# State-space input stage: softplus as one activation from PSUM, du per chunk, constants first, loops written out

## The reference

```
# state-space block (m0 and m1), 256 inner channels, 16 states
u, z    = split(x @ W_in)
u       = silu(causal_conv4(u))
dt,B,C  = split(u @ W_x)                     # 8, 16, 16 columns
delta   = softplus(dt @ W_dt + b_dt)
A       = -exp(A_log)
h[t]    = exp(delta[t]*A) * h[t-1] + delta[t]*u[t]*B[t]
y[t]    = sum over states of h[t]*C[t]  + u[t]*D
out     = (y * silu(z)) @ W_out

# mixture of experts (e0 and e1), 8 experts, the best 2 of each token
topv, topi = top_k(x @ Wg.T, 2);  w = softmax(topv)
comb       = one_hot(topi) weighted with w   # [tokens, 8]
```

## Time and profile before

| | us |
|---|---|
| median of three executions | 2250.76 |
| the profiled execution's own time | 2255.21 |
| its span, first to last instruction | 2253.4 |
| TensorE busy | 1847.1 (82%) |
| VectorE busy | 1723.9 (77%) |
| ScalarE busy | 1102.9 (49%) |
| GpSimd busy | 463.3 (21%) |
| granted TensorE clock, mean | 0.926 |

### The profile page before, as it was taken

The page is one execution under the profiler, slowest core; times in us unless marked ns, Lnnn a source line. Parts: engine busy times, 40 slices in busy tenths (PEclk is TensorE's granted clock), DMA queues, the critical chain, the costliest instruction groups (busy, mean ns, idle before and its releaser), DMA issues. The chain is left out here.

```text
span 2253.4 us, 48041 instructions
## 1 busy us (share of the span) xinstructions
PE 1847.1 (82%) x18116; PEld 897.4 (40%) x18116; DVE 1723.9 (77%) x3657; ACT 1102.9 (49%) x2023; POOL 463.3 (21%) x342
## 2 busy tenths in 40 slices
PE   6377777999479999998699964777685999999957
PEld 2122235344235555554434321222342555555524
DVE  5999975555679999993655469999766899999745
ACT  5433322322328778787222263333152777887825
POOL 2566641000200000000100025766431000000012
PEclk9699998999769999999799987999886999999978
DMA  3121201000111222212100001212003132222110
GB/s 104 42 82 67 82 30 57 1 0 0 56 47 41 51 52 52 46 36 34 58 0 0 0 8 49 84 65 78 25 1 106 26 55 60 52 50 50 30 16 19
DMA packets 43053, 96.50 MB, mean 43 GB/s; under 512 B 14153, under 2 KB 18189, under 8 KB 41438
## 3 DMA queue, kind: packets, MB, share of 16 engines
q1 hardware_dynamic: 41694, 91.04, 15.7%
q10 hardware_dynamic: 1152, 2.64, 0.3%
HBM read 75.42 MB, written 17.04 MB: 41 GB/s over the span
## 5 line engine op out<-in xcount | busy, mean ns | idle before, releaser
L1805 ACT ACTIVATE a1hd_probs<-a1hd_ps_k 128x512 f32<-128x512 f32 (+3 forms) x640 | 302.2, 543 | 118.2 <-PE a1hd_ps_k L1703 79.1
L1805 ACT ACTIVATE a0hd_probs<-a0hd_ps_k 128x512 f32<-128x512 f32 (+3 forms) x640 | 302.3, 543 | 117.0 <-PE a0hd_ps_k L1703 79.8
L1685 PE MATMUL a0hd_ps_q<-a0hd_k_op,a0hd_q_op 72*32 72x512 bf16 (+3 forms) x2560 | 270.5, 368 | 27.9 <-DMA a0hd_k_op<-a_k_parts 18.1
L1685 PE MATMUL a1hd_ps_q<-a1hd_k_op,a1hd_q_op 84*32 84x512 bf16 (+3 forms) x2560 | 270.3, 368 | 27.8 <-DMA a1hd_k_op<-in_alibi_k 18.1
L1763 DVE TENSOR_REDUCE a0hd_maxes<-a0hd_ps_q 128x1 f32<-128x512 f32 x384 | 252.1, 685 | 24.8 <-PE a0hd_ps_q L1685 21.7
L1763 DVE TENSOR_REDUCE a1hd_maxes<-a1hd_ps_q 128x1 f32<-128x512 f32 x384 | 252.2, 685 | 24.6 <-PE a1hd_ps_q L1685 21.2
L1699 PE MATMUL a1hd_ps_k<-a1hd_q_op,a1hd_k_op 87*32 87x512 bf16 (+3 forms) x2560 | 262.5, 352 | 7.4 <-ACT a1hd_probs L1805 4.9
L1699 PE MATMUL a0hd_ps_k<-a0hd_q_op,a0hd_k_op 75*32 75x512 bf16 (+3 forms) x2560 | 262.2, 352 | 6.5 <-ACT a0hd_probs L1805 4.9
L1033 ACT ACTIVATE e_silu<-e_psg,e_me_b 128x512 f32<-128x512 f32 x128 | 87.9, 687 | 256.7 <-PE e_psg L947 256.7
L1146 DVE SCALAR_TENSOR_TENSOR e_mid<-e_psv,e_me_b,e_silu 128x512 f32<-128x512 f32 x128 | 95.8, 750 | 108.6 <-PE e_psv L949 104.8
L608 POOL TENSOR_TENSOR m1sc_read<-m1sc_state,m1sc_c_rows 128x1024 f32<-128x1024 f32 x64 | 150.1, 2356 | 76.8 <-DVE m1sc_state L580 51.5
(11 more groups left out here) (349 smaller groups left out, 3322.7 us busy)
## 6 DMA issues: line engine op xcount, KB each, us to landing
m0sc_c_rows<-m_c_rows SPq DMA_DIRECT2D x32, 512.0 KB, 3.5
m1sc_c_rows<-m_c_rows SPq DMA_DIRECT2D x32, 512.0 KB, 3.6
a_oT<-a_outputs SPq DMA_DIRECT2D x32, 256.0 KB
a0hd_q_op<-a_q_parts SPq DMA_DIRECT2D x16, 288.0 KB
a0hd_k_op<-a_k_parts SPq DMA_DIRECT2D x16, 288.0 KB
a_outputs<-a0hd_o_sb SPq DMA_DIRECT2D x256, 18.0 KB
a1hd_q_op<-a_q_parts SPq DMA_DIRECT2D x16, 288.0 KB
a1hd_k_op<-a_k_parts SPq DMA_DIRECT2D x16, 288.0 KB
```

Of the source, the lines that this page charges most:

```text
L1685: last = pe.matmul(ps_q[32 * r:32 * r + 32, bank, 0:width], q_op[k % SLOT][0:NR, part(t, r)], k_op[k % SLOT][0:NR, kc * CH:kc * CH + width ...
L1805: act.activation(probs[:, n % PSLOT, 0:width], ps_k[:, n % KB, 0:width], ACT.Exp).then_inc(exp_done, 1)
```

## The change

In `mamba_inputs`:

- delta is one ScalarE activation, Softplus with the bias, straight from the dt bank, per chunk and channel half. `e`, the absolute value, max(dt,0), exp, ln, the rounding remainder and all additions to delta are gone, on all three engines.
- The dt products stand at the end of `items`: both halves of chunks 0 and 1, the xd product of chunk 3, then chunks 2 and 3. ScalarE does softplus of chunk 0 in step 5 ahead of the xd copy of chunk 3, and those of chunks 1, 2 and 3 after the steps, with the second bf16 part of chunk 3 between 1 and 2.
- du is made by VectorE alone, one product per chunk (1024 elements per partition).
- exp(A_log) is ScalarE's first instruction; its negation and the two instructions for diag_d stand in VectorE's step 0, behind the first normalisation.
- The DRAM rows hold B and C (32 rows a chunk, not 16); the scan reads the C rows from row 16 on.

In `mamba_scan` the loops are written out: the same steps in the same order on each engine, with constant targets and slices. In `moe` the loop over chunks is written out too, and the choice of experts is made by comparisons over all 2048 tokens at once: equal to the best value, times a row 8..1, maximum over the experts, equal to that row; the second with one more comparison that takes the first out. The row `iota` holds 8..1 in place of 0..7.

```diff
 def mamba_inputs(...)
-        for s in range(STEPS):
+        for s in range(NC + 1):
             items += [("u", s, h) for h in range(NH2) if s < NC]
-            items += [("dt", s - 3, h) for h in range(NH2) if s >= 3]
-            items += [("xd", s - 2, 0)] if 2 <= s < NC + 2 else []
-            items += [("gate", s - 1, h) for h in range(NH2) if 1 <= s <= NC]
-        late = {"u": 0, "gate": 1, "xd": 2, "dt": 3}
-        reader = {"u": raw_copied, "xd": xd_ready, "dt": relu_done, "gate": gate_ready}
+            items += [("xd", s - 2, 0)] if s >= 2 else []
+            items += [("gate", s - 1, h) for h in range(NH2) if s >= 1]
+        items += [("dt", c, h) for c in range(2) for h in range(NH2)]
+        items += [("xd", NC - 1, 0)]
+        items += [("dt", c, h) for c in range(2, NC) for h in range(NH2)]
+        reader = {"u": raw_copied, "xd": xd_ready, "dt": delta_ready, "gate": gate_ready}
...
 scalar
+            def second(c):
+                act.wait_ge(rest_ready, c + 1)
+                act.activation(parts[:, 1, chunk(c)], rest[:, c % 2, :], ACT.Copy).then_inc(split_1, 1)
+            def softplus(c):
+                for h in range(NH2):
+                    act.wait_ge(made, product_made("dt", c, h))
+                    act.activation(delta[:, h, chunk(c)], bank("dt", c, h), ACT.Softplus,
+                                   bias=w["dt_b"][:, h:h + 1]).then_inc(delta_ready, 1)
             act.wait_ge(w.loaded, w.full)
-            for s in range(STEPS):
+            act.activation(neg_a[:, :, :], w["a_log"][:, :, :], ACT.Exp).then_inc(a_exp, 1)
+            for s in range(NC + 2):
...
-                if s >= 3:
-                    ... Abs of dt (2 halves), second part of chunk s-3
+                if s >= 3 and s < NC + 2:
+                    second(s - 3)
+                if s == NC + 1:
+                    softplus(0)
...
-            ... exp of both halves, ln of both halves
+            softplus(1)
+            second(NC - 1)
+            softplus(2)
+            softplus(3)
 vector
                 if s == 0:
                     dve.wait_ge(padded, 1)
                     dve.wait_ge(w.loaded, w.full)
+                    dve.wait_ge(a_exp, 1)
+                    link(dve.tensor_scalar(neg_a[:, :, :], neg_a[:, :, :], -1.0, None, ALU.mult))
+                    for h in range(NH2):
+                        link(dve.tensor_scalar(diag_d[:, h, :], g["ident"][:, :], w["d"][:, h:h + 1], None, ALU.mult))
...
-            ... relu of dt, neg_a, diag_d, round_sum, lost_in_rounding, delta + ln, times_u(1)
+            for c in range(NC):
+                dve.wait_ge(delta_ready, NH2 * (c + 1))
+                dve.tensor_tensor(du[:, :, chunk(c)], delta[:, :, chunk(c)], u[:, :, chunk(c)], ALU.mult).then_inc(du_ready, 1)
 gpsimd
-                if s == NC + 1:
-                    lost_in_rounding(pool, 0)
-            times_u(pool, 0)
 sync
-                sp.dma_start(c_dram[:, chunk(c)], xd[RANK + NS:XDBL, chunk(c)]).then_inc(c_stored, 16)
+                sp.dma_start(bc_dram[:, chunk(c)], xd[RANK:XDBL, chunk(c)]).then_inc(c_stored, 16)

 def mamba_scan(...)
-            with eng.Fori(1, NS // 2) as i:
-                for s in range(2):
-                    step(k, i + k * (NS // 2), s)
+            for q in range(STEPS):          # on every engine, constant waits and slices
...
 def moe(...)
-                for i in range(NT):
-                    dve.wait_ge(maxed, i + 1)
-                    dve.max_index(index[:, i, :], best[:, i, :], logits[:, i, :]).then_inc(indexed, 1)
+            def find_index(k, marks):
+                last_first = g["iota"][:, :].unsqueeze(1).broadcast_to([P, NT, NE])
+                link(dve.tensor_tensor(marks[:, :, :], logits[:, :, :], spread(best[:, :, k:k + 1], NE), ALU.is_equal))
+                if k:
+                    link(dve.tensor_tensor(marks[:, :, :], marks[:, :, :], is0[:, :, :], ALU.is_gt))
+                link(dve.tensor_tensor(marks[:, :, :], marks[:, :, :], last_first, ALU.mult))
+                link(dve.tensor_reduce(rank[:, :, k:k + 1], marks[:, :, :], AX.X, ALU.max))
+                link(dve.tensor_tensor(marks[:, :, :], last_first, spread(rank[:, :, k:k + 1], NE), ALU.is_equal))
...
-            find_index()
+            find_index(0, is0)
             make_mid(0, 4, 4)
             make_mid(0, 5, 5)
-            mark()
+            find_index(1, is1)
...
-            with pe.Fori(1, NC - 1) as c:   # the same on scalar and vector
-                body(c, True)
-            body(NC - 1, False)
+            for c in range(1, NC):
+                body(c, c + 1 < NC)
```

More of the change, by code:

```diff
@@ L283, in _ @@
             pe.wait_ge(w.loaded, w.full)
-            for s in range(STEPS):
-                if s < NC:
-                    norm.turn(pe, s)
-                for k, (what, c, h) in enumerate(items):
-                    if c + late[what] != s:
-                        continue
+            for k, (what, c, h) in enumerate(items):
+                    if what == "u" and h == 0:
+                        norm.turn(pe, c)
                     if k >= RING:
@@ L325, in _ @@
                                        ACT.Copy).then_inc(raw_copied, 1)
-                if s >= 3:
-                    c = s - 3
-                    for h in range(NH2):
-                        act.wait_ge(made, product_made("dt", c, h))
-                        act.activation(e[:, h, chunk(c)], bank("dt", c, h), ACT.Abs,
-                                       bias=w["dt_b"][:, h:h + 1]).then_inc(abs_done, 1)
-                    act.wait_ge(rest_ready, c + 1)
-                    act.activation(parts[:, 1, chunk(c)], rest[:, c % 2, :], ACT.Copy).then_inc(split_1, 1)
+                if s >= 3 and s < NC + 2:
+                    second(s - 3)
+                if s == NC + 1:
+                    softplus(0)
                 if 2 <= s < NC + 2:
@@ L460, in _, with mamba_scan @@
             sp.wait_ge(g.late.loaded, g.late.full)
-def mamba_scan(nc, g, tag, u, delta, du, bc3, c_dram, neg_a, diag_d, gate):
+def mamba_scan(nc, g, tag, u, delta, du, bc3, bc_dram, neg_a, diag_d, gate):
     with ExitStack() as ctx:
@@ L485, in mamba_scan, with time, rows @@
         NB = SCT // CH
+        STEPS = NSC * NS
         block = ctx.enter_context(nc.Block())
[L488 to L506 removed]
+        def time(q, first=0, last=SCT):
+            return slice(q // NS * SCT + first, q // NS * SCT + last)
         @block.tensor
         def _(pe):
[L510 to L511 removed]
+            def rows(q):
                 for h in range(NH2):
[L513 removed]
+                    if q:
+                        pe.wait_ge(scanned, NH2 * (q - 1) + h + 1)
                     for b in range(NB):
[L515 to L517 removed]
+                        last = pe.matmul(drive[:, h, chunk(b)], g["sel"][:, q % NS, :], bc3[:, time(q, b * CH, (b + 1) * CH)],
+                                         start=True, stop=True)
+                    last.then_inc(rows_spread, 1)
             def skip(k):
@@ L529, in sum_states @@
                     for b in range(NB):
-                        last = pe.matmul(psy[:, h, chunk(b)], g["ident"][:, :], read[s][:, h, chunk(b)],
-                                         start=False, stop=ends, skip_group_check=True)
+                        last = pe.matmul(psy[:, h, chunk(b)], g["ident"][:, :], read[q % 2][:, h, chunk(b)],
+                                         start=False, stop=q % NS == NS - 1, skip_group_check=True)
                     last.then_inc(summed, 1)
-            def middle(k, r, s):
-                rows(k, r, s)
-                sum_states(r * 2 + (s - 1), 1 - s, False)
@@ L586, in times_gate @@
                     dve.wait_ge(summed, NS * NH2 * (k + 1) - (NH2 - 1 - h))
-                    dve.tensor_tensor(gate[:, h, tokens], psy[:, h, :], gate[:, h, tokens], ALU.mult).then_inc(gated, 1)
-            step(0, 0, 0)
-            for k in range(NSC):
-                step(k, k * (NS // 2), 1)
-                other_pairs(dve, k, step)
-                if k + 1 < NSC:
-                    step(k + 1, (k + 1) * (NS // 2), 0)
-                times_gate(k)
+                    dve.tensor_tensor(gate[:, h, time(NS * k)], psy[:, h, :], gate[:, h, time(NS * k)], ALU.mult).then_inc(gated, 1)
@@ L612, in _ @@
         @block.sync
         def _(sp):
[L614 to L619 removed]
+            for q in range(STEPS):
+                if q >= 2:
+                    sp.wait_ge(read_ready, NH2 * (q - 1))
+                sp.dma_start(c_rows[q % 2][:, :], bc_dram[NS + q % NS:NS + q % NS + 1, time(q)].broadcast_to([P, SCT])).then_inc(c_loaded[q % 2], 16)
@@ L926, in tokens @@
             def tokens(c):
-                return chunk(c) if isinstance(c, int) else ds(c * CH, CH)
+                return chunk(c)
             def product(c, e):
@@ L1059, in _ @@
             tail(0, True)
-            with act.Fori(1, NC - 1) as c:
-                body(c, True)
-            body(NC - 1, False)
```

(7 more changed lines are left out.)

185 lines of the change are left out of this document (47 added, 138 removed).

## The result

The changed kernel takes 2200.59 us, median of four executions (2200.30 to 2204.75), against 2250.14 for four of the kernel before on the same chip. The ratio is 0.978, with a 95% interval of 0.977 to 0.980. The forecast was 2197.7 in a range of 2191 to 2209; its sum had said 53.1 us, and the gain is 49.5 by the medians, 50.5 by the two profiled executions (own time 2204.75, span 2202.9). The mechanism and the place were right; one term, the block of m1, was 4 us too large.

A forecast was written before the change was run, and what follows sets the result against it. VectorE was taken to bound the input block's end. Savings of 25.5 + 25.5 + 1.0 - 0.45 + 1.6 = 53.1 us, against the median 2250.8, gave 2197.7; the 8-in-10 range was 2191 to 2209.

The forecast's parts named there:

- The place: End of the input block: VectorE, running without a gap from 62.04 to 87.98, was said to hold up the scan.
- The end of the block, m0: Input block of m0: to end at 62.4 instead of 87.98, 25.5 us less.
- the working: Part-by-part costing of the input block's new end; SiLU of chunk 3 to start of scan came to 12.8 us.
- The end of the block, m1: Input block of m1: the same 25.5 us less, as it repeats m0 row by row.
- dt 0, dt 1, xd 3 at 1.95 each: TensorE near the block's end: three products in turn from 49.4, 1.95 us each, done at 55.2.
- the stacking DMA: End of the input block: stacking of B and C lands last, at 62.4, 0.6 us behind du.
- Softplus, 1.28 a pair: ScalarE in the input block: a softplus pair costs 1.28 us, as the absolute value of the same shape did.
- Rival 1: Input block's end: ScalarE becomes the bound, by two-pass Softplus (+7) or extra table loads (+10); 2205 to 2208, chance 0.10.
- The starts: Start of the input blocks: exp(A_log) first moves table loads, gaining 1.0 us in m0 and losing 0.45 in m1.
- The experts: Expert layers e0 and e1: TensorE's 0.78 us wait for the mid product goes, 0.8 a layer, 1.6 together.
- The loops: Scan and experts: writing the loops out gains 0 us, register arithmetic being hidden by VectorE.
- Rival 2: Stages after the input block: without TensorE's rest before each scan the granted clock drops, costing 10 us; 2208, chance 0.05.

The follow-up runs named there:

- after_again: The changed kernel run once more with nothing edited; 2202.9 us.
- e6: The changed kernel with the dt products from bf16 operands, lower parts of dt left out; 2199.02 us, ratio 0.976.
- e4: The kernel before with only exp(A_log), its negation and diag_d moved to the start of the input block; 2245.88 us, ratio 0.9975.
- e5_repeat: The changed kernel with xd of chunk 3 ahead of the dt products of chunk 1; first run 2199.91 us, this second run 2198.11.
- e2: The kernel before with only the choice of experts made by comparisons; 2249.77 us, ratio 0.999.
- e1: The kernel before with only the loops of scan and experts written out; 2248.88 us against 2250.73, ratio 0.999.
- e3: The changed kernel with exp(A_log) behind the last softplus, negation and diag_d behind the last du, in both layers; 2204.8 us, ratio 0.980.

## Why the prediction was right, point by point

- **The place.** VectorE's unbroken stretch at the end of the two input blocks was the bound, and it goes: 26.0 + 21.0 of the 50.5 us lie in the two blocks (81.0 to 55.0, 76.2 to 55.2).
- **The end of the block, m0, 25.5 predicted; right in sum, by two errors that cancel.** With the start the block was to lose 26.5 and lost 26.0. The front was 3.7 better than the working: the SiLU of chunk 3 came 6.4 earlier (44.4 to 38.0 after the block's start), not 2.75. In the kernel before the clock had fallen in that front, and in this run of the changed one it had not. TensorE's rows for the u products of chunk 2 and xd of chunk 0, before and after:

```profile
28.23 2.50 PE L297 MATMUL m0in_acc<-m0in_xT,all_m_in_T 128*128 128x512 f32 x4 [2.69 <-ACT m0in_xT L189]
30.66 3.01 PE L301 MATMUL m0in_acc<-m_u,all_m_x_T 128*40 128x512 f32 x4
```

```profile
25.42 1.96 PE L284 MATMUL m0in_acc<-m0in_xT,all_m_in_T 128*128 128x512 f32 x4 [1.24 <-ACT m0in_xT L188]
27.31 1.91 PE L288 MATMUL m0in_acc<-m_u,all_m_x_T 128*40 128x512 f32 x4
```

This is 1.6 of it. The second run of the changed kernel, with a fall of the clock there, has 41.0, which is 0.65 below the 41.65 of the working. The tail was 4.2 worse (17.0, not 12.8), because TensorE ran at 0.50. That the block came out right to 0.5 is luck: the working had neither.
- **The end of the block, m1, 25.5 predicted; this is the term that was mis-sized.** With the start, 25.05 was to go, and 21.0 did. Here the fall of the clock is new in the front (SiLU of chunk 3 at 40.6, not 38.2; in the run without it, after_again, 38.0), and the tail is 14.6, not 12.8: 2.4 + 1.8. Of the clock the working took TensorE's rows from a stretch at 1.00. The step that failed is "dt 0, dt 1, xd 3 at 1.95 each"; measured are 4.62 for the first two, 3.64 for the third in m0. The prediction also says that m1 repeats m0 row by row. That holds from the SiLU of chunk 3 on (36.6 to the scan in both); the front of m1 was 39.5 and that of m0 44.4.
- **What ends the block.** I named the stacking DMA. In m1 it fits: VectorE's last du ended at 1326.90 and its first instruction of the scan came 1.34 later, 2.35 after the last stacking issue, as in e6. In m0 it is not: the last du ended at 61.98 and the memset followed 0.36 later. Dt of chunk 3 came so late from TensorE that du passed the DMA.
- **Softplus, 1.28 a pair.** Measured 679 ns mean in m0, 673 in m1, pairs of 1.24 to 1.27 where TensorE doesn't hold them. Rival 1 falls on both counts: one pass, and no load between the softplus calls, though Copy stands there.
- **The starts.** M0: 1.35 gained, not 1.0 (first copy at 11.51, not 12.86). The load didn't wait for the weights; it ran at 7.24, ahead of the wait for them. M1: 0.45 predicted, and right where the clock came up early: the copy of the third transposed chunk came 17.37 after the block's start, not 16.96 as before, and e4, the kernel before with the same loads at the start, has it at 17.37 too. Where TensorE stays at the lower level longer, as in e5_repeat, the same load costs 1.25.

```profile
7.24 1.28 ACT L309 ACT_TABLE_LOAD   x1 [7.24 <-PEq L1936]
8.93 0.23 ACT L309 ACTIVATE m_neg_a<-all_m_a_log 128x32 f32<-128x32 f32 x1 [0.41 <-DMA all_m_out_T<-in_m_out_T]
```

- **A load has no drain behind it.** In the rows of after the load of 46.95 ends at 48.23 and softplus follows at 48.25; the one at 7.24 lay in a wait altogether. The Trainium skill, "ScalarE: Activation LUTs", section "What ACT_TABLE_LOAD costs", adds 1.38 us to each; these rows contradict it, as those of before did.
- **The experts, 1.6 predicted.** The stretch with e0 lost 1.0 and that with e1 0.2 in the profiles: 1.2, and e2 agrees for e0; the 0.2 is not told apart from noise. TensorE's first mid product after the choice comes at 369.89 with no wait for VectorE.
- **The loops, 0.** Right: e1.
- **Not of the change.** 2.3 us came in m1's scan, which lasts 227.9 and not 230.2. It is not the change: two kernels with the old input blocks, e2 and e4, have 228.1 and 227.8 there, e5 in its first run 230.1. VectorE waits there for TensorE where the halves meet and at the end: 3.88 and 4.34 before, with the clock at 0.62 and 0.56 just ahead of it, and 2.60 and 3.34 after, at 0.97 and 1.00. The span's 50.5 are thus 47.0 of the two blocks, 1.2 of the experts, 2.4 of the two scans by the clock, and 0.1 lost behind them.
- **Rival 2, the clock gives some back**, had 0.05 and came nearest to what was missing, though at another place: not in the stages after the scan, which are no longer than before in this profile, but in the block itself, where TensorE had become what ScalarE waits for.

## What to carry to other kernels

A long row beside a working GpSimd is no price of its operation: taking the row out moves the wait to the next one, and only taking GpSimd's operation out removes it. When an edit shortens a block that one engine bound, cost the new end also with TensorE at its lower level, and put the product that the longest chain hangs on (here xd of the last chunk) first in its list: that order gave 2.5 to 4 us in the block of m0 and 1.4 to 2 in that of m1. A table load belongs where the engine waits anyway, which was worth 1.35 us in m0; that it should stand next to the other user of its function is not shown, for in m1 the gain was between nothing and 0.5 us.

## What the runs showed of the hardware that was not expected

**TensorE fell to its lower level within unbroken work.** In the kernel before it worked from 37.9 to 54.9 us without a pause at the full clock, of which this is a part:

```profile
38.00:50.00 12.00, 12.00 (x26) 3.79 (x27) 7.95 (x10) 9.73 (x18) 3.82 (x3) 1.00 0.05 12
```

In the changed kernel its last idle time in the block ended at 40.96, and it fell at 47.4. In all runs of the changed form, the one with bf16 dt among them, in which TensorE rests from 54 us on (0.85 from 49 to 54, 0.50 after), the clock falls at some point of the tail. From the end of that idle time to the first matmul of double length it is 6.4 to 7.9 us in the eight blocks of the changed kernel and of e3, and 10.1 to 11.7 in the six blocks with xd of chunk 3 first. What decides where is open; the experiments show what it costs, and that with the other order it falls later and ScalarE waits less for it. The same fall, for some 4 us, comes and goes in the fronts of both blocks from run to run, worth up to 3 us each.

**VectorE held by GpSimd, to the end of the instruction.** The rows of e4 above fit one account: the rounded sum issued at 61.54 ends at 64.97, which is GpSimd's end at 59.38 + 4.51 = 63.89 plus nearly its own 1.23; the remainder from 65.00 ends at 71.48, which is GpSimd's 63.97 + 5.37 = 69.34 plus 2.29, less 0.15; GpSimd's sum, 4.50 alone, took 5.37 because it waited for the rounded sum's end; and its third part, 1.15 alone, then took 3.20, to 72.49, one microsecond behind VectorE's end. By the same sum neg_a of before, 3.38 from 62.04, ends 0.03 behind GpSimd's 60.88 + 4.51. The Trainium skill, "SBUF — State Buffer", section "Who interferes with whom", describes the port pair of these two engines as a lock that is held for the whole instruction, the other engine blocking fully; it names operations with two SBUF inputs and those in a two-port mode, which tensor_scalar can enter. The rows agree: the rounded sum, with one input, took 1.23 for 2048 elements where the two-input remainder took 2.29, and was held like it.
